# Attention of layer 1: which engine masks which group of keys, and who divides by the sums

## The reference, cut to what matters

```python
def _L1_xattn_ref(query, key, value, mask, ...):      # 256 queries, 4096 keys, 16 heads of 16
    q = split_heads(query @ wq_kernel + wq_bias)
    k = split_heads(key @ wk_kernel + wk_bias)
    v = split_heads(value @ wv_kernel + wv_bias)
    scores = jnp.einsum('bhqd,bhkd->bhqk', q, k) / jnp.sqrt(jnp.float32(HD))
    scores = jnp.where(mask[:, None, :, :] == 0, jnp.float32(-1000000000.0), scores)
    attn = jax.nn.softmax(scores, axis=-1)
    out = jnp.einsum('bhqk,bhkd->bhqd', attn, v)
    return out.transpose(0, 2, 1, 3).reshape(b, -1, D) @ wo_kernel + wo_bias
```

## Time and profile before

| | before |
|---|---|
| median of 3 executions | 1391.3 us (1388.78 to 1392.65) |
| profiled execution, its own time | 1390.09 us |
| span of its trace | 1388.9 us |
| mean granted TensorE clock | 0.954 of full |
| busy: PE, DVE, ACT, POOL | 1239.3, 1004.7, 845.6, 532.7 us |
| 556 to 785 us (this stage, 229 us): PE, DVE, ACT, POOL busy | 214.6, 172.6, 174.5, 101.1 us |

### The profile page before, as it was taken

One profiled execution on the slowest core, in us unless ns is written; L12 is line 12 of the kernel. 1 busy time (PEld: TensorE's weight loads), 2 busy tenths in 40 slices (PEclk: granted clock), 3 DMA queues, 4 the chain that ended last, 5 costly groups with the idle time before them and its releaser, 6 DMA issues. The chain is left out here.

```text
span 1388.9 us, 29847 instructions
## 1 busy us (share of the span) xinstructions
PE 1239.3 (89%) x10867; PEld 625.2 (45%) x10942; DVE 1004.7 (72%) x2294; ACT 845.6 (61%) x1329; POOL 532.7 (38%) x822
## 2 busy tenths in 40 slices
PE   7899988999998788799999888789999896999987
PEld 6466642333333366133333455334444583444445
DVE  4868689999998435888888153489995247999931
ACT  4632238999998330488888542258888211888862
POOL 1531317888899602444444231033232001232310
PEclk9999987999999979699999999979999997899999
DMA  8699960111122020212114154412226201222400
GB/s 303 204 327 312 334 224 22 39 42 49 47 83 65 1 76 3 67 41 57 55 43 141 49 155 148 132 52 59 70 78 209 77 0 43 58 59 73 124 1 8
DMA packets 115316, 136.47 MB, mean 98 GB/s; under 512 B 13721, under 2 KB 96607, under 8 KB 113118
## 3 DMA queue, kind: packets, MB, share of 16 engines
q1 hardware_dynamic: 107282, 126.47, 29.3%
q10 hardware_dynamic: 7888, 8.09, 1.8%
HBM read 99.57 MB, written 34.90 MB: 97 GB/s over the span
## 5 line engine op out<-in xcount | busy, mean ns | idle before, releaser
L1359 ACT ACTIVATE prob_a<-ps 128x1024 f32<-128x1024 f32 x480 | 471.6, 1020 | 84.5 <-PE ps L1171 42.3
L1151 PE MATMUL ps<-kop,qop 52*128 52x512 f16 x1024 | 284.4, 410 | 42.5 <-DVE best_a L1385 22.9
L1385 DVE TENSOR_REDUCE best_a<-ps 128x1 f32<-128x512 f32 (+1 forms) x486 | 314.8, 711 | 9.0 <-PE ps L1151 6.3
L1171 PE MATMUL ps<-qop,kop 52*128 52x256 f16 x2048 | 230.6, 280 | 2.6 <-ACT prob_a L1359 1.2
L1200 PE MATMUL ps<-prob_a,vop_a 128*32 128x256 f32 x3072 | 208.3, 390 | 0.8 <-ACT folded_sums_a L1303 0.7
L1381 DVE CUSTOM_DVE_ANT_0 dump_a<-ps,neg_q 128x512 bf16<-128x512 f32 (+1 forms) x244 | 165.8, 715 | 34.8 <-PE ps L1151 33.5
L1151 PEld LDWEIGHTS ps<-kop,qop 52*128 52x128 f16 x1024 | 72.9, 95 | 220.8 <-DVE best_a L1385 85.5
L1501 POOL TENSOR_TENSOR used_a<-prob_a,gT 128x1024 f32<-128x1024 f32 x64 | 154.0, 2408 | 23.3 <-DVE used_a L1398 18.2
L1171 PEld LDWEIGHTS ps<-qop,kop 52*128 52x128 f16 x2048 | 84.7, 96 | 102.6 <-issue 40.7
L1479 POOL TENSOR_SCALAR mrest_a<-nmax_a 128x2 f32<-128x2 f32 x64 | 28.1, 439 | 245.7 <-DVE nmax_a L1390 225.5
L1200 PEld LDWEIGHTS ps<-prob_a,vop_a 128*32 128x32 f32 x3072 | 81.7, 110 | 87.7 <-issue 52.8
(11 more groups left out here) (405 smaller groups left out, 1759.0 us busy)
## 6 DMA issues: line engine op xcount, KB each, us to landing
kop<-kparts SPq DMA_DIRECT2D x384, 64.0 KB, 2.3
vals<-vst SPq DMA_DIRECT2D x16, 1024.0 KB, 6.3
kparts<-kp SPq DMA_DIRECT2D x64, 256.0 KB, 5.1
vraw<-vals SPq DMA_DIRECT2D x64, 256.0 KB, 3.0
e_w<-in_e_w SPq DMA_DIRECT2D x4, 2048.0 KB, 10.9
z_w<-in_z_w SPq DMA_DIRECT2D x24, 256.0 KB, 6.3
gT<-in_ctxT SPq DMA_DIRECT2D x8, 512.0 KB, 12.4
raw<-in_mask SPq DMA_DIRECT2D x16, 256.0 KB, 4.1
```

Source lines behind the costliest of these rows:

```text
L1151: return pe.matmul(out, qop[rows, h, t * P:(t + 1) * P], kop[rows, h % UNROLL, first:first + CHUNK], start=True, stop=True)
L1171: ins = pe.matmul(st_bank(n)[:, j * NT:(j + 1) * NT], kop[rows, h % UNROLL, at:at + P], qop[rows, h, :], start=(j % 2 == 0), stop=(not add ...
L1359: act.activation(prob[:, n % NP, :], st_bank(n), ACT.Exp, scale=1.0 / SCORE_UNIT).then_inc(S("exp_done"), 1)
L1385: dve.tensor_reduce(out, bank, AX.X, ALU.max).then_inc(sem, 1)
```

## The change

Of the eight groups of a head, groups 0 and 4 are now masked by GpSimd, group 2 by VectorE, and 1, 3, 5, 6 and 7 by M on TensorE (one M fewer for each head). The bounding pass of ScalarE is gone: the exponential is taken straight from PSUM, and the bound is put on the result instead. GpSimd does this in a pass of its own ahead of the multiplication, `min` with 1 and `max` with 0, in place on 128 x 1024; VectorE has `min` and the multiplication in one instruction (step W, semaphore "capped"). The division of heads 0 to 14 goes to GpSimd. `AHEAD` grows from 24 to 26 chunks, the order string, `SUM_AT` and `TURN_AT` are new. `find_seen` is written with two operators (multiply, add) in place of one comparison, and is done for three groups, the third behind `split(0)`. In GpSimd's loop the place of `shield` for groups beyond the second moves, which changes nothing with two groups.

```diff
-MASKED_ORDER = "CCKKCCV CCKKCCCV CKKCF CTKCCV KCCV".replace(" ", "")
+MASKED_ORDER = "V CCKKCCV KCCKC FCCKKCC W K T CKCCV V CC".replace(" ", "")
...
-    AHEAD = 32 if weighted else 24 if by_query else 26
+    AHEAD = 32 if weighted else 26
...
-    SUM_AT, TURN_AT = (1, 1) if weighted else (3, 4) if by_query else (3, 4)
-    SHIELD = (1, 5) if l == SHIELDED else ()
+    SUM_AT, TURN_AT = (1, 1) if weighted else (1, 5) if by_query else (3, 4)
+
+    SHIELD, BOUNDED, CAPPED = ((0, 4), (), (2,)) if l == SHIELDED else ((), (), ())
...
-    aside = lambda h: not by_query and h < H - 1
+    aside = lambda h: not weighted and h < H - 1
...
-            elif (n - 2) % NGROUP in SHIELD:
-                pe.wait_ge(S("bounded"), shields(n - 2) + 1)
+            elif (n - 2) % NGROUP in BOUNDED:
+                pe.wait_ge(S("bounded"), bounds(n - 2) + 1)
...
-                added = by_query and g not in SHIELD and g not in own
+                added = by_query and g not in SHIELD and g not in CAPPED and g not in own
...
+            elif g in CAPPED:
+                pe.wait_ge(S("capped"), h + 1)
...
-                if g in SHIELD:
+                if g in BOUNDED:
                     act.activation(prob[:, n % NP, :], st_bank(n), ACT.Relu, scale=-1.0).then_inc(S("bounded"), 1)
...
+                elif step == "W" and CAPPED:
+                    n = NGROUP * h + CAPPED[0]
+                    dve.wait_ge(S("exp_done"), n + 1)
+                    if h == 0:
+                        dve.wait_ge(S("seen_found"), 2 * len(SHIELD + CAPPED))
+                    dve.scalar_tensor_tensor(out=prob[:, n % NP, :], in0=prob[:, n % NP, :], scalar=1.0,
+                                             in1=seen(CAPPED[0]).rearrange("p k q -> p (k q)"), op0=ALU.min, op1=ALU.mult)\
+                       .then_inc(S("capped"), 1)
...
-            pool.tensor_scalar(seen(g), seen(g), 0.0, None, ALU.is_equal).then_inc(S("seen_found"), 1)
+            pool.tensor_scalar(seen(g), seen(g), -1.0 / NEG, 1.0, ALU.mult, ALU.add).then_inc(S("seen_found"), 1)
...
+            if g not in BOUNDED:
+                pool.tensor_scalar(prob[:, n % NP, :], prob[:, n % NP, :], 1.0, 0.0, ALU.min, ALU.max).then_inc(S("lowered"), 1)
+                pool.wait_ge(S("lowered"), (len(SHIELD) - len(BOUNDED)) * h + [i for i in SHIELD if i not in BOUNDED].index(g) + 1)
             pool.tensor_tensor(prob[:, n % NP, :], prob[:, n % NP, :], seen(g).rearrange("p k q -> p (k q)"), ALU.mult)\
                 .then_inc(S("shielded"), 1)
...
-            for i, g in enumerate(SHIELD):
+            for i, g in enumerate(SHIELD[:2]):
                 find_seen(i, g)
         split(0)
+        if l == SHIELDED:
+            for i, g in enumerate((SHIELD + CAPPED)[2:]):
+                find_seen(i + 2, g)
```

More of the change, by code:

```diff
@@ L1076, in attend @@
     rden = sb("rden", [P, 2, QT], F32)
-    folded_sums = None if by_query else sb("folded_sums", [P, 2, QT, 32], F32)
-    minus_one = None if by_query else sb("minus_one", [P, QT], F32)
+    folded_sums = None if weighted else sb("folded_sums", [P, 2, QT, 32], F32)
+    minus_one = None if weighted else sb("minus_one", [P, QT], F32)
     dump = sb("dump", [P, 1, CHUNK] if weighted else [P, 2, 2 * CHUNK], BF16) if by_query else None
@@ L1100, in attend @@
     summed = lambda h, t, j: FIRST + SC // 2 * (h - 2) + len(own) * t + own.index(j) + 1
+    bounds = lambda n: len(BOUNDED) * (n // NGROUP) + BOUNDED.index(n % NGROUP)
+    seen = lambda g: c.neg_k[:, g * GROUP:(g + 1) * GROUP, :]
     shields = lambda n: len(SHIELD) * (n // NGROUP) + SHIELD.index(n % NGROUP)
@@ L1281, in _ @@
         stage.reads = slots.n
-        stage.divided = 0 if by_query else H - 1
+        stage.divided = 0 if weighted else H - 1
     @stage.scalar
@@ L1353, in _ @@
                     act.wait_ge(S("pv_psum"), n - NP + 1)
-                if g in SHIELD:
+                if g in BOUNDED:
                     act.activation(prob[:, n % NP, :], st_bank(n), ACT.Relu, scale=-1.0).then_inc(S("bounded"), 1)
-                    act.wait_ge(S("bounded"), shields(n) + 1)
+                    act.wait_ge(S("bounded"), bounds(n) + 1)
                     act.activation(prob[:, n % NP, :], prob[:, n % NP, :], ACT.Exp, scale=-1.0 / SCORE_UNIT).then_inc(S("exp_done"), 1)
@@ L1409, in normalise @@
                 dve.wait_ge(S("den_added"), h + 1)
-            if not by_query:
+            if not weighted:
                 dve.wait_ge(S("divided"), H - 1)
             dve.reciprocal(rden[:, h % 2, :], den[:, h % 2, :] if weighted else folded[:, :, HD]).then_inc(S("den_inverted"), 1)
-            dve.wait_ge(S("den_inverted"), h + 1 if by_query else 1)
+            dve.wait_ge(S("den_inverted"), h + 1 if weighted else 1)
             dve.tensor_tensor(c.att[:, :, HD * h:HD * (h + 1)], folded[:, :, 0:HD],
@@ L1533, in gather @@
             pool.tensor_tensor(others[:, h % 2, :], pairs[:, :, 0], pairs[:, :, 1], ALU.add).then_inc(S("gathered"), 1)
-        seen = lambda g: c.neg_k[:, g * GROUP:(g + 1) * GROUP, :]
         def find_seen(i, g):
-            pool.tensor_scalar(seen(g), seen(g), 0.0, None, ALU.is_equal).then_inc(S("seen_found"), 1)
+            pool.tensor_scalar(seen(g), seen(g), -1.0 / NEG, 1.0, ALU.mult, ALU.add).then_inc(S("seen_found"), 1)
             pool.wait_ge(S("seen_found"), 2 * i + 1)
@@ L1547, in shield @@
             pool.wait_ge(S("exp_done"), n + 1)
-            if h == 0 and g == SHIELD[0]:
-                pool.wait_ge(S("seen_found"), 2 * len(SHIELD))
+            if h == 0:
+                pool.wait_ge(S("seen_found"), 2 * (SHIELD.index(g) + 1))
+            if g not in BOUNDED:
+                pool.tensor_scalar(prob[:, n % NP, :], prob[:, n % NP, :], 1.0, 0.0, ALU.min, ALU.max).then_inc(S("lowered"), 1)
+                pool.wait_ge(S("lowered"), (len(SHIELD) - len(BOUNDED)) * h + [i for i in SHIELD if i not in BOUNDED].index(g) + 1)
             pool.tensor_tensor(prob[:, n % NP, :], prob[:, n % NP, :], seen(g).rearrange("p k q -> p (k q)"), ALU.mult)\
@@ L1600, in _ @@
                 fill(h + 1)
+            for g in SHIELD[2:]:
+                shield(h, g)
             if h + 1 < H and HALVES_SET < HALVES:
@@ L1604, in _ @@
                 divide(h - 1)
-            for g in SHIELD[2:]:
-                shield(h, g)
     return stage
```

## The result

| | before | after |
|---|---|---|
| median | 1391.45 us (20 executions, 1386.28 to 1398.93) | 1395.99 us (20 executions, 1391.10 to 1416.92) |
| ratio | | 1.0027, 95% interval 1.0016 to 1.0038 |
| span of the profiled execution | 1388.9 us | 1394.1 us |
| mean granted clock | 0.954 | 0.954 |
| the stage (its warm-up product to the first product behind its last fold) | 544.49 to 783.01: 238.52 us | 546.59 to 787.08: 240.49 us |

The changed kernel is slower by a quarter of a per cent; its execution of 1416.92 us, at a granted clock of 0.904, stands apart from the other nineteen (up to 1398.96) and is left out of the ratio. Of the 5.2 us between the two spans, 2.0 lie in the stage. The rest lies ahead of it (2.1) and behind it (1.1), where the code is the same. The stage is what the change can explain, so I compare its length from here on.

What follows compares the result with a forecast made beforehand. TensorE in its written order was taken to bound the stage. 13 heads x 0.90 = -11.7 and -1.5 for start and end took 1390.1 to 1376.9; with the median 1.2 higher, the forecast was 1378 us, range 1372 to 1396.

Steps and rivals of the forecast that it cites:

- What bounds the kernel before: Old stage: TensorE in its written order is the bound, its steps summing to 13.11 us a head against 13.18 measured.
- the price of TensorE's steps: TensorE, start to start: 0.11 a run, 0.213 a unit, M 0.53, V 1.00, F 0.56, T 0.21; new head 12.24.
- M, runs, ScalarE and the division: Per head: M's fall to 5, runs from 12 to 9; ScalarE's lost passes give nothing; division takes 0.4 off VectorE.
- The pass: GpSimd's min/max on 1024 columns: taken as 1.2 us, inside 1.03 to 1.63, with outer bounds 1.0 and 3.1.
- turning point: Pass duration d in each head: from 1.2 us on W starts first; at 1.03 GpSimd's multiplication does.
- The race: Each head: W at 8.78 against GpSimd's group 4 multiplication at 7.58 + d; the later one stands still.
- that case: Rival, GpSimd's multiplication starts first: TensorE stands for 1.0, head 13.4 us, kernel 1392.5 us; chance 0.30.
- What GpSimd's pass waits for: GpSimd's pass for group 4 starts 0.08 us behind exponential 4, which ends at 7.42 in the head.
- Start and end: Stage outside 13 steady heads: -1.4 - 1.1 - 1.0 + 1.15 + 0.4 + 0.5 = -1.5 us.
- Sign and size: Whole kernel: faster, forecast 1378 us; chances faster 0.57, same 0.28, slower 0.15.
- W first: Likeliest case, W starts before GpSimd's multiplication and nothing stalls: head 12.28 us, kernel 1373 to 1383 us; chance 0.47.
- the multiplication first: Rival, W waits for GpSimd's multiplication and ends at 11.9 in the head: +0.2 us a head, 1392.5 us; chance 0.30.

Runs made afterwards that it cites:

- gp_nudge: Changed kernel plus a pause, a small memset on GpSimd between min/max pass and multiplication, for groups 0 and 4: 1376.10 us, ratio 0.9889 to the kernel before.
- nudge_second: Changed kernel with the small GpSimd memset between pass and multiplication for group 4 only: 1378.98 us, ratio 0.9895 to the kernel before.
- w_one_input: Changed kernel with W replaced by a maximum reduction over the same tile, group 2's cap and mask left out: 1373.40 us, ratio 0.9853 to the kernel before.
- nudge_two_passes: gp_nudge with ScalarE's bounding passes put back for groups 6 and 7: 1379.21 us, ratio 0.9920 to the kernel before.
- nudge_dve_divides: gp_nudge with the division by the sums given back to VectorE: 1388.12 us, ratio 0.9975 to the kernel before.
- memset_ahead: Changed kernel with a small GpSimd memset in front of each wait for the exponential: 1380.80 us, ratio 0.9906 to the kernel before.
- gp_nudge_again: Repeat of gp_nudge, the changed kernel with both small GpSimd memsets: 1380.48 us, ratio 0.9893 to the kernel before.
- gp_waits: Changed kernel with GpSimd's multiplication of group 4 made to wait for W by semaphore: 1379.82 us, ratio 0.9921 to the kernel before.
- w_early: Changed kernel with W one chunk earlier in the order string: 1389.04 us, ratio 0.9984 to the kernel before.

## Why the prediction was wrong

- **What bounds the kernel before, and the price of TensorE's steps: right.** The sum gave 12.24 and 12.28 with small waits. The five runs in which neither W nor V of groups 4 and 5 is late (both gp_nudge runs, nudge_second, w_one_input, nudge_two_passes) show 12.09. The old head (13.11 by the same prices, 13.18 measured) and the new one are thus off by 0.5% and 1.2%. TensorE is busy for the whole of the new one (12.09 in gp_nudge). The gain itself, 1.09 a head, was put at 0.90. Two joins that the prices left out make up the difference: two V's in a row take 1.87 and not 2.00 (644.39 to 646.26 in gp_nudge), and T behind an M takes 0.65 with it and not 0.74 (654.43 to 655.08).
- **M, runs, ScalarE and the division: right, mostly.** Five M's and joined C C K K steps are worth 1.1 us a head. ScalarE's lost passes are worth nothing there (nudge_two_passes). I costed the division on VectorE by its busy time, 0.4, and took it for hidden. Taking it back costs 0.7 a head, since F then takes a ring bank (nudge_dve_divides); the prediction doesn't have that bank in its sum, and VectorE's 11.3 of a head were right (11.46 above).
- **The pass: the step that failed.** The mechanism was right and one term of it, the duration d of the min/max pass, was mis-sized. I took 1.2, "inside 1.03 to 1.63", although the scaling of L912 with a fixed part gave 1.03. It measured 1.04 to 1.05. My own sum had the turning point at 1.2: below it the multiplication is first. The prediction put the value exactly on the edge and let it fall on the side with the gain. With the measured value the multiplication is first, W takes 3.10 and not 1.22, TensorE waits for it once a head, and the head is 13.50 and not 12.28.
- **The race: mechanism right, side wrong.** I forecast W at 8.78 and the multiplication at 7.58 + d. With d = 1.04 that is 8.62, W late by 0.16; measured 0.11. The other rival times of that case hold too: V delayed by 1.0 and the C's by 0.1 (1.2 and 0.2 measured), head 13.4 (13.50), time 1392.5 (1395.99).
- **What GpSimd's pass waits for: incomplete.** I counted it from exponential 4. In the changed kernel `split` ends at about the same time (648.04 in the head shown), and the pass stands behind both, so whatever is added on GpSimd there moves the race (memset_ahead).
- **Start and end: half right.** I had -1.5 for all that lies outside thirteen steady heads. In gp_nudge the stage is 12.0 shorter than before, and 13 x (13.18 - 12.09) = 14.2, so the ends cost 2.2 there. TensorE waits 1.85 for `split` ahead of the second T, with the granted clock at 0.57 from 579 to 587 us (0.82 before). With the pause for group 4 only, the stage is shorter by 4.1 and 2.8 than in the two executions with both, and the ends give 1.9, close to the 1.5 of the forecast. With one trace for each kernel these differences between the ends stay open.
- **Sign and size.** The sign was wrong: 1395.99 lies on the very edge of the range of 1372 to 1396, on the side of the loss. With W first the change is worth 12 to 16 us in the stage and about 1.1% in all, close to the forecast 1378; with the multiplication first it costs 0.3%. The chances were 0.47 to 0.30, for a difference of 0.17 us that I had called hardly more than I could vouch for.

gp_nudge, gp_nudge_again and nudge_second beat both kernels. The gain of all three rests on a lead of about 0.1 us, and nothing in them forces the order; gp_waits does force it, and keeps 0.8%.

## What to carry to other kernels

When two engines read SBUF in each head and one of them is on the path, write down the two starts, not the two durations: 0.1 us decided 1.4 us a head here. If the estimate puts the turning point on your chosen value, the forecast is a coin toss, and the change should be built so that the order is forced, or so that the engine off the path starts later. And look at who starts last in a race before you save work there: a pass of 1.04 us in place of the 1.2 of the forecast lost this one.

## What the runs showed of the hardware

- One operator costs more than two on GpSimd, for the same tile. `min` alone took 2.77 us on 128 x 1024 fp32, `min` and `max` 1.04. `find_seen` points the same way in bf16, though there the operators differ too: the comparison alone took 2.87, multiply and add take 1.05 to 1.09 (timeline of GpSimd, changed kernel):

```profile
554.40 1.09 POOL L1550 TENSOR_SCALAR neg_k<-neg_k 128x1024 bf16<-128x1024 bf16 x1
```

- The one that starts first runs undisturbed whatever the margin: seen with leads from 0.02 to 0.12 us. The other ends nearly as late as if it had begun behind it (W 1.08 behind the multiplication's end, the multiplication 2.01 behind W's): W 3.10 to 3.20 in place of 1.22, the multiplication 3.13 in place of 2.13.
- GpSimd's pass, which reads one tensor, holds VectorE's two-input instruction too (w_early: 1.50 in place of 1.22, its end 1.08 behind the pass's). A VectorE reduction of the same tile is not held.
- A held instruction holds others in its turn. In the changed kernel W runs at last when the multiplication has ended, and GpSimd's next read, `fill`'s copy, then takes 1.61; with the pause it takes 0.61.
